# Delta-rule layer: the diagonal blocks copied out inside the substitution, and four programs written in another order

## The reference, cut to what matters

```python
def step(S, inp):                       # over the N = 256 tokens; 4 heads of 32
    q_t, k_t, v_t, b_t = inp
    pred = jnp.einsum('bhk,bhkv->bhv', k_t, S)
    err = (v_t - pred) * b_t[..., None]
    S = S + jnp.einsum('bhk,bhv->bhkv', k_t, err)
    o_t = jnp.einsum('bhk,bhkv->bhv', q_t, S)
    return (S, o_t)
q = _l2norm(split(x @ Wq, Dk)); k = _l2norm(split(x @ Wk, Dk)); v = split(x @ Wv, Dv)
beta = jax.nn.sigmoid(x @ Wbeta)
o = _delta_rule(q, k, v, beta)
o = o * rsqrt(mean(o * o) + 1e-5) * g_norm      # per head
x = x + o @ Wo
```

## Time and profile before

| | us |
|---|---|
| median of 3 runs | 4800.96 (4797.86 to 4804.31) |
| the profiled execution | 4797.98 |
| its span in the profile | 4796.2 |
| granted TensorE clock, mean over the span | 0.923 |
| DVE busy | 3511.9 (73%) |
| PE busy | 4027.6 (84%) |

### The profile page before, as it was taken

The page is one execution under the profiler, slowest core; times in us unless marked ns, Lnnn a source line. Parts: engine busy times, 40 slices in busy tenths (PEclk is TensorE's granted clock), DMA queues, the critical chain, the costliest instruction groups (busy, mean ns, idle before and its releaser), DMA issues.

```text
span 4796.2 us, 66046 instructions
## 1 busy us (share of the span) xinstructions
PE 4027.6 (84%) x15980; PEld 2235.2 (47%) x15980; DVE 3511.9 (73%) x11308; ACT 3084.9 (64%) x5650; POOL 1555.8 (32%) x2846
## 2 busy tenths in 40 slices
PE   4478757999999999999999999994878649999965
PEld 2266643444444444444444444442555436666644
DVE  4588658888878878788787887785656956565578
ACT  1355425999989888889898898993122225555532
POOL 1222122444444444444444444443001013333310
PEclk9688778999999999999999999997999769999987
DMA  1011101000000000000000000000000001111100
GB/s 54 18 23 23 27 0 22 1 18 5 1 21 3 15 10 1 19 5 1 24 1 15 10 1 19 5 1 0 0 0 0 0 15 41 40 41 41 41 1 18
DMA packets 132031, 69.71 MB, mean 15 GB/s; under 512 B 92345, under 2 KB 124814, under 8 KB 129316
## 3 DMA queue, kind: packets, MB, share of 16 engines
q1 hardware_dynamic: 124020, 52.62, 4.5%
q10 hardware_dynamic: 7600, 12.58, 0.7%
HBM read 52.39 MB, written 12.80 MB: 14 GB/s over the span
## 4 chain that ended last, share of the span: by engine, by line
PE 44%; DVE 20%; ACT 15%; issue 12%; DMA 3%; POOL 3%; ACTq 1%; SPq 1%; DVEq 0%; POOLq 0%
PE bank L1807 11%; PE bank L1822 6%; PE bank L1851 4%; PE bank L2576 4%; ACT arena L1902 3%; DMA packed_dram<-arena 2%; PE bank L1861 2%; ACT arena L1911 2%; ACT arena L2036 2%; DVE arena L2011 2%; ACT arena L1898 2%; PE bank L643 2%; PE bank L2609 2%; ACT arena L1899 2%; DVE arena L1988 2%
## 5 line engine op out<-in xcount | busy, mean ns | idle before, releaser
L1807 PE MATMUL bank<-arena 128*128 128x512 f32 x3072 | 1416.0, 594 | 12.8 <-DVE arena L1988 11.6
L1807 PEld LDWEIGHTS bank<-arena 128*128 128x128 f32 x3072 | 584.3, 190 | 751.7 <-issue 726.7
L2048 POOL TENSOR_SCALAR arena<-arena 128x256 f32<-128x256 f32 x1024 | 511.8, 510 | 1079.3 <-DVE arena L1981 1076.9
L1822 PE MATMUL bank<-arena 128*128 128x512 f32 x1024 | 528.9, 608 | 59.6 <-DVE arena L2011 58.3
L2011 DVE SCALAR_TENSOR_TENSOR arena<-arena 128x256 f32<-128x256 f32 x1024 | 530.7, 557 | 0.0
L1970 DVE SCALAR_TENSOR_TENSOR arena<-arena 128x256 f32<-128x256 f32 x1024 | 391.1, 418 | 179.6 <-ACT arena L1899 179.6
L1988 DVE SCALAR_TENSOR_TENSOR arena<-bank,bv,arena 128x256 f32<-128x256 f32 x1024 | 444.9, 472 | 0.0
L1898 ACT ACTIVATE arena<-bank,bqk 128x512 f32<-128x512 f32 x512 | 348.9, 681 | 108.1 <-PE bank L1807 98.6
L1981 DVE SCALAR_TENSOR_TENSOR arena<-bank,bq,arena 128x512 f32<-128x512 f32 x512 | 384.3, 751 | 18.0
L1911 ACT ACTIVATE arena<-arena,const_table 128x512 f32<-128x512 f32 x512 | 374.7, 732 | 0.0
L2587 DVE TENSOR_REDUCE arena<-bank 128x2 f32<-128x512 f32 x256 | 176.3, 689 | 250.6 <-PE bank L2578 250.5
(11 more groups left out here) (372 smaller groups left out, 7565.1 us busy)
## 6 DMA issues: line engine op xcount, KB each, us to landing
arena<-packed_dram SPq DMA_DIRECT2D x48, 192.0 KB
arena<-packed_dram ACTq DMA_DIRECT2D x16, 576.0 KB
arena<-diag_dram SPq DMA_DIRECT2D x16, 256.0 KB, 3.9
arena<-in_L_attn_Wk_dram SPq DMA_DIRECT2D x16, 256.0 KB, 3.2
arena<-in_L_attn_Wq_dram SPq DMA_DIRECT2D x16, 256.0 KB, 4.0
arena<-in_L_attn_Wv_dram SPq DMA_DIRECT2D x16, 256.0 KB, 4.3
arena<-in_L_attn_Wo_dram SPq DMA_DIRECT2D x8, 512.0 KB, 3.8
arena<-in_L_attn_W_dram SPq DMA_DIRECT2D x16, 256.0 KB, 3.1
```

The source lines that it names most:

```text
L1807: nc.tensor.matmul(bank[:, RING1[m % 5], :], w1p[k][:, i * P:(i + 1) * P], zT_of(g), start=True, stop=True).then_inc(a1_proj.sem, 1)
L1822: nc.tensor.matmul(bank[:, 6, :], wo1[:, i, :], a1_att[:, i % 4, :], start=(i == 0), stop=(i == NB1 - 1)).then_inc(a1_outd.sem, 1)
L2048: last = nc.gpsimd.tensor_scalar(a, a, 1.0, a1_ksum[:, i % 4, b:b + 1], ALU.add, ALU.mult)
```

## The change

Nothing is computed differently. The edits are:

- `a0_os`, the squares of the output, now lies in the memory of `a0_prod` (the products of the substitution) and no longer in `a0_kb`; the waits follow from that.
- On DVE a slot now begins with the first three rows of the substitution (`HEAD_ROWS`, rows 30 to 28) and `turn_blocks_dve`, and only then come `mask_dve` and `square_out_dve`. `norm_out_dve` stands directly behind `squares_dve`, `unit_dve` behind row 13, `apply_dve` behind it, and `diag_dve` between row 5 and row 4.
- On ACT `spread_act` stands ahead of `keep_act`, `it6_act` ahead of `turn_act`, `agram_act` behind the first `err_act`, and the query copies ahead of `o_act`.
- On PE `turn_pe` stands behind `it6_pe` and `agram_pe` behind the first `err_pe`.
- The lists of POOL and SP are unchanged.

```diff
@@ attn0 set-up
+            a0_os = a0_prod.rearrange("p (q d) -> p q d", q=QT)
             a0_kb = a0_Itc.rearrange("p s c -> p (s c)").rearrange("p (q d) -> p q d", q=QT)
-            a0_os = a0_kb
+            HEAD_ROWS = range(DK0 - 2, DK0 - 5, -1)
@@ substitute_dve
                         a0_sub.wait(nc.vector, g, k)
+                        if r == HEAD_ROWS[-1] - 1 and g >= 2:
+                            a0_osq.wait(nc.vector, g - 2)
@@ turn_blocks_dve
                 nc.vector.wait_ge(a0_xloaded, 16 * (g + 1))
-                if g >= 1:
-                    a0_osq.wait(nc.vector, g - 1)
@@ square_out_dve
                 if g + 2 < G:
-                    a0_turned.wait(nc.vector, g + 2)
+                    a0_sub.wait(nc.vector, g + 2, 2 * (DK0 - 2 - HEAD_ROWS[-1]) + 4)
@@ program_pe
-                    + both(x6_pe) + [(4, out_turn_pe), (1, turn_pe)] + both(it6_pe) + [(4, out_pe), (1, agram_pe)]
-                    + both(lambda b: err_pe(b, 0)) + both(state_pe)
+                    + both(x6_pe) + [(4, out_turn_pe)] + both(it6_pe) + [(1, turn_pe), (4, out_pe)]
+                    + both(lambda b: err_pe(b, 0)) + [(1, agram_pe)] + both(state_pe)
@@ program_act
-                    [(1, keep_act), (3, spread_act)] + both(x5_act)
+                    [(3, spread_act), (1, keep_act)] + both(x5_act)
...
-                    + [(0, with_parity(copy_act))] + both(lambda b: err_act(b, 1)) + both(o_act)
-                    + [(2, heads_act(0, a0_zq))])
+                    + [(0, with_parity(copy_act))] + both(lambda b: err_act(b, 1))
+                    + [(2, heads_act(0, a0_zq))] + both(o_act))
@@ program_dve
-                    [(0, with_parity(stats_dve)), (3, mask_dve), (4, square_out_dve), rows(30, 28), (3, turn_blocks_dve),
-                     rows(27, 23), (1, squares_dve), rows(22, 16), (0, with_parity(apply_dve)), (1, unit_dve),
-                     (4, norm_out_dve), rows(15, 0), (1, diag_dve), (4, add_dve)])
+                    [(0, with_parity(stats_dve)), (2, substitute_dve(HEAD_ROWS)), (3, turn_blocks_dve), (3, mask_dve),
+                     (4, square_out_dve), rows(HEAD_ROWS[-1] - 1, 22), (1, squares_dve), (4, norm_out_dve), rows(21, 13),
+                     (1, unit_dve), (0, with_parity(apply_dve)), rows(12, 5), (1, diag_dve), rows(4, 0), (4, add_dve)])
```

More of the change, by code:

```diff
@@ L1619, in program_act @@
                 over_slots(
-                    [(1, keep_act), (3, spread_act)] + both(x5_act)
+                    [(3, spread_act), (1, keep_act)] + both(x5_act)
                     + [(3, i21_act(0)), (3, it5_act(0)), (3, i21_act(1)), (3, it5_act(1))]
-                    + both(x6_act) + [(4, out_act), (1, turn_act), (1, heads_act(2, a0_zk))] + both(it6_act) + [(1, agram_act)]
-                    + both(lambda b: err_act(b, 0)) + both(state_act) + both(rest_act)
-                    + [(0, with_parity(copy_act))] + both(lambda b: err_act(b, 1)) + both(o_act)
-                    + [(2, heads_act(0, a0_zq))])
+                    + both(x6_act) + [(4, out_act)] + both(it6_act) + [(1, turn_act), (1, heads_act(2, a0_zk))]
+                    + both(lambda b: err_act(b, 0)) + [(1, agram_act)] + both(state_act) + both(rest_act)
+                    + [(0, with_parity(copy_act))] + both(lambda b: err_act(b, 1))
+                    + [(2, heads_act(0, a0_zq))] + both(o_act))
             def program_dve(e):
```

## The result

| | before | after |
|---|---|---|
| median | 4802.64 us (4 runs, 4797.86 to 4804.57) | 4853.72 us (4 runs, 4834.42 to 4869.81) |
| profiled execution, its span | 4797.98, 4796.2 | 4834.42, 4832.6 |
| delta-rule stage, from its first eviction on ScalarE to the next stage's first | 149.36 to 639.73: 490.4 | 148.96 to 685.29: 536.3 |
| waits of VectorE in it: for the query-key products | 57.9 | 20.7 |
| for POOL's power of the output | 7.2 | 50.8 |

The changed kernel is slower, ratio 1.0104 [1.008, 1.0129]. The forecast was 4850, the range 4829 to 4864.

The account below looks back on a forecast made before the run. A slot was taken as VectorE's work plus its starting wait for matmuls. Terms 8.1 + 42.9 + 0.3 - 2.0 = 49.3 us on 4797.98 give 4847.3; on the median, 4850, range 4829 to 4864.

Parts of the forecast that it names:

- copy-out's wait, slots 4 to 8: VectorE's copy-out of the diagonal blocks waits for copies of the key products: 1.2 us a slot, between 0 and 3.1.
- slot 9: No sums of squares here, so POOL serves the output at once: 44.2 us against 43.9, 0.3 more.
- Scaling of the output: VectorE, slots 4 to 8: idles 9.0 us because POOL computes the sums' power before the output's.
- Start, head, masks: Slot start on VectorE: load until 6.3 us, masks 5.2; sums of squares begin at 19.5 instead of 23.1, gaining 3.6.
- Slots 2 and 3: Slot 2 ends at 226.7; slot 3 takes 49.35 us and ends at 276.05, 8.1 later than before.
- Slot 10: Transposes no longer stand behind masks; of ACT's 4.77 us wait, 2.0 us comes off, between 0 and 4.8.
- PE and ACT at nothing: List moves on TensorE and ScalarE cost nothing, covered by VectorE's waits; uncovered, worth up to 57.9 us.
- The late products: First rival: slow TensorE products make the copy-out wait 3.1 us and masks 1.7 a slot; 4868 us, chance 0.09.
- The short start: Second rival: load at 5.1 us and masks at 3.9, slots 3 to 9, no copy-out wait; 4826 us, chance 0.08.
- third rival: POOL's powers do not hold VectorE's output scaling, slots 4 to 8: 45 us less, 4805 us, chance 0.03.
- The rule on shared interfaces: Skill rule that POOL contends with VectorE would shorten powers beside idle VectorE; the prediction kept its row of 5.4 us.

Follow-up runs that it names:

- masks_first: Changed kernel with POOL's output power ahead of the sums-of-squares power, and VectorE's masks and output squares ahead of the memsets: 4796.68 us, ratio 0.9996.
- new_pe_act: Kernel before with only the TensorE and ScalarE lists of the changed kernel: 4810.48 us, ratio 1.0024.
- the old lists: Changed kernel with the TensorE and ScalarE lists of the kernel before: 4846.29 us, ratio 1.008.
- the short program: Kernel before and changed kernel, both cut to the first three of twelve stages: 615.85 and 673.63 us.
- pool_out_first: Changed kernel with POOL's power of the output moved ahead of its power of the sums of squares: 4799.98 us, ratio 0.9992.
- keep_first: masks_first with keep_act ahead of spread_act again on ScalarE: 4768.78 us, ratio 0.9939.
- the other four: Four more runs of the changed kernel, unchanged: 4849.26 us, ratio 1.0105.

## Why the prediction was right, step by step

| step | predicted | measured in the profile after |
|---|---|---|
| load of the blocks behind the issue of the inverse | 6.3 | 6.31 |
| four masks | 5.2 | 5.2 |
| idle ahead of the scaling of the output | 9.0 in slots 4 to 8 | 8.80 in each |
| copy-out's wait, slots 4 to 8 | 1.2 (0 to 3.1) | 0.81, 1.00, 0.97, 1.02, 2.03 |
| five slots, end of row 0 to end of row 0 | 308.1 | 306.95 (inverse issues 276.39 to 583.34) |
| end of slot 3 | +8.1 | +8.9 |
| slot 9 | +0.3 | +0.2 |
| slots 10 and 11 | -2.0 (0 to -4.8) | -4.8 |
| sum of the stage | +49.3 | +46.0 |

**Scaling of the output.** Right in mechanism and size, and shown by taking it away: with POOL's order mended the wait and 44 us are gone. The prediction charged the slot 9.0 us because nothing stands between the sums of squares and the scaling; that the whole loss hung on it came out as written. One premise was too short: VectorE did have other long waits, for the adding to x (16.6), the key products (12.3), the last output (11.8) and the load (9.9). They stand at the stage's two ends, outside slots 4 to 8, so the sum did not suffer.

**Start, head, masks.** Right to a tenth of a us. What the prediction did not draw from it is that the start itself is a loss to be had back: VectorE idles 4.5 us for a load while four masks stand behind it. With POOL's order mended, that and the evictions' place were worth 27 us of the stage (492.1 to 465.2).

**Slots 2 and 3.** 0.8 too short, as the rest of two misses. Slot 2 ended 1.4 us earlier than forecast (225.26 for 226.7; 0.4 of that is the stage's earlier start), since from the unit scaling to the last copy of the key products it took 12.4 us and not the 13.45 carried over. Slot 3 took 51.1 us (inverse issues 225.26 to 276.39) and not 49.35: its copy-out waited 1.21 us, where the sum charged a wait only from slot 4 on, and the sums of squares waited 0.44 us for ScalarE's last eviction, which the prediction did not look for. This last is the small end of the waits of 4.98 us in masks_first and 5.69 in new_pe_act.

**Slot 10.** Mis-sized: the 4.77 us of the earlier trace rows were taken at 2.0 because the combining products should have followed the query-key products. All of it came back.

**PE and ACT at nothing.** Right for the stage (536.9 against 536.3 with the old lists), in part by luck: about 1 us a slot against the new lists and 5 us of another clock at the end cancel. And "worth up to the 57.9 us" named a bound without its other side: in the kernel before the new lists lose 11.1 us of the stage.

**The late products.** The chance was for all slots; it happened in three slots of the short program, where the copy-out waited 3.4 us longer than in a good slot, in one of pool_out_first, and in neither profile of the changed kernel. The prediction reasoned from the work that TensorE has there (the error products in between); in the two stretches compared above the work is the same, and the granted clock is what differs. The short start and the third rival did not occur.

**The rule on shared interfaces.** The power beside an idle VectorE took 5.42 us, as the prediction's row said, so the rule did not shorten it. In pool_out_first and keep_first, however, where POOL begins the power just as VectorE scales the output, it takes longer. Timeline of VectorE, then of POOL, in slot 7 of keep_first:

```profile
432.36 0.68 DVE L1567 TENSOR_TENSOR arena<-arena 128x512 f32<-128x512 f32 x1
```

```profile
432.52 5.79 POOL L1178 TENSOR_TENSOR arena<-arena,const_table 128x32 f32<-128x32 f32 x1 [4.50 <-DVE arena L1173]
```

5.79 to 5.80 us in slots 4 to 8, 5.45 in slots 2 and 3, which have no output to scale. The Trainium skill (GPSIMD Engine Reference, Key points) says that POOL contends with VectorE's instructions that read two inputs from SBUF, as this scaling does; the 0.37 us fit that, though no run tested them alone. The products of the substitution read two inputs from SBUF as well, and the power beside them took 5.43 us in the kernel before: these rows do not show the contention that the section would lead one to expect there.

**The medians.** The forecast's 4850 stands 3.7 from the first four runs (4853.72) and 0.7 from the other four. That nearness is partly luck. The eight runs spread from 4834.42 to 4872.36, about as wide as the range, and two of the first four (4866.32 and 4869.81) lie above its end of 4864; the prediction had no term for a spread that comes from outside the edited stage. The stage gave 46.0 us where 49.3 were forecast, and the medians moved by 51.1. The profiled execution was the fastest of the eight. It ended 36.4 us behind the one of before and not 46, since its stages outside the delta stage took 4296.3 us and not 4305.8; 7.0 of that is the last attention stage.

## What to carry to other kernels

An instruction moved to where its engine has time needs its producer moved too: look up in the other engine's list what stands ahead of the producer, and when the input of that comes. A wait read off a profile is worth its full length only if no other wait stands behind it; here the same moves on TensorE and ScalarE were worth 24 us, nothing in sum, or a loss of 11, by what VectorE's and POOL's lists were. And when an edit leaves an engine waiting for a transfer, put the work that is ready there, and check which engine's queue that transfer holds up next.

## What the runs showed of the hardware

POOL's power on 128x32 elements takes 5.42 us, on 128x16 2.90 and on 128x4 1.01; VectorE takes 0.69 us for a product of 128x512. In the shortened kernel, after 5.4 us of idling TensorE's granted clock was 0.55 in mean over one stretch of turns and key products and 0.76 over the same stretch two slots later; the copy-out waited 3.4 us longer in the first. In the last slot the products of the last output ran at 0.91 in one profile and at 0.59 in another, and VectorE waited 10.6 and 15.6 us for them. The order of one list moved the stage by 44 us with no instruction added or removed.
